# Values of one pair of heads after each round in the last five groups of attention

## What is computed

```python
def _L0_attn_ref(x, w_qkv, w_out, b_out):       # x: (8, 512, 256), H = 16
    qkv = x @ w_qkv
    q, k, v = jnp.split(qkv, 3, axis=-1)
    ...                                         # heads, rotation of q and k
    dots = jnp.einsum('bhid,bhjd->bhij', q, k) * scale
    attn = jax.nn.softmax(dots, axis=-1)
    out = jnp.einsum('bhij,bhjd->bhid', attn, v)
    ...
    return out @ w_out + b_out
x = x + _layernorm(_L0_attn_ref(_layernorm(x, axis=-1), ...), axis=-1)
x = x + _layernorm(_L0_ffn_ref(_layernorm(x, axis=-1), ...), axis=-1)
```

## Time and profile before

| | |
|---|---|
| time, median of 3 runs | 923.57 us (922.79 to 928.46) |
| the profiled execution | 924.53 us, span 921.5 us |
| mean granted TensorE clock | 0.945 |
| busy in the span | PE 777.2 us, DVE 654.4, ACT 519.5, POOL 377.2 |
| attends | 128, from 81.5 to 557.05 us |
| groups 27 to 31, from the last attend of group 26 | from 490.17 us |

### The profile page before, as it was taken

How to read it: one execution, slowest core, us unless ns; L and a number is a source line. 1 busy time by engine, 2 the same in 40 slices (tenths; PEclk the granted TensorE clock), 3 DMA queues, 4 the chain that set the end, 5 groups by cost and what they waited for, 6 DMA issues and landing times. The chain is left out here.

```text
span 921.5 us, 14947 instructions
## 1 busy us (share of the span) xinstructions
PE 777.2 (84%) x4690; PEld 482.1 (52%) x4690; DVE 654.4 (71%) x1252; ACT 519.5 (56%) x1050; POOL 377.2 (41%) x446
## 2 busy tenths in 40 slices
PE   4478899999999999999968877999999788888784
PEld 3344334344443344433422335787787688887673
DVE  4367778888888787987868844777875355554685
ACT  2214566767667676677747763434342376665363
POOL 4350071361632714418101010456566067666442
PEclk9657899999999999999979997999999899999998
DMA  8584925847739468286563401345447546556994
GB/s 154 115 223 96 221 48 128 192 112 146 161 101 196 93 145 191 95 173 116 130 170 59 185 1 49 98 144 161 150 156 220 144 136 183 170 171 204 283 174 91
DMA packets 112420, 133.27 MB, mean 145 GB/s; under 512 B 16724, under 2 KB 80726, under 8 KB 112344
## 3 DMA queue, kind: packets, MB, share of 16 engines
q1 hardware_dynamic: 99096, 109.18, 48.1%
q0 software_dynamic: 13248, 23.15, 9.7%
HBM read 68.18 MB, written 59.87 MB: 139 GB/s over the span
## 5 line engine op out<-in xcount | busy, mean ns | idle before, releaser
L460 DVE TENSOR_REDUCE negmax<-ring 128x2 f32<-128x1024 f32 x256 | 307.1, 1212 | 82.9 <-PE ring L615 81.5
L413 ACT ACTIVATE probs<-scores 128x512 f32<-128x512 f32 x498 | 272.3, 601 | 74.6 <-PE scores L631 73.5
L631 PE MATMUL scores<-q_st,k_st 64*128 64x512 f32 x498 | 208.2, 471 | 42.4 <-ACT probs L413 36.3
L615 PE MATMUL ring<-k_st,q_st 48*128 48x512 f32 x512 | 182.7, 469 | 9.2 <-DMA k_st<-rows_in 4.8
L631 PEld LDWEIGHTS scores<-q_st,k_st 64*128 64x128 f32 x498 | 83.0, 187 | 183.1 <-ACT probs L413 131.9
L643 PE MATMUL av<-probs,v_aug 128*32 128x512 f32 x1024 | 139.0, 615 | 6.3 <-ACT probs L413 6.3
L318 POOL CAST part_r<-negmax 128x16 fp32r<-128x16 f32 x32 | 8.4, 262 | 189.0 <-DVE negmax L460 189.0
L615 PEld LDWEIGHTS ring<-k_st,q_st 48*128 48x128 f32 x512 | 69.8, 193 | 16.8 <-DVE negmax L460 8.1
L1485 POOL DMA_INDIRECT rows_out<-m_y,projected x48 | 47.3, 985 | 45.7 <-ACT m_y L1550 35.1
L564 PE MATMUL misc<-projected,t_hi 128*128 128x512 f32 (+1 forms) x236 | 64.8, 365 | 0.0
L1636 DVE TENSOR_TENSOR m_h_lo<-scores,m_h_hi 128x512 fp32r<-128x512 f32 x40 | 27.7, 691 | 51.4 <-ACT m_h_hi L1536 51.3
(11 more groups left out here) (240 smaller groups left out, 1678.7 us busy)
## 6 DMA issues: line engine op xcount, KB each, us to landing
q_st<-rows_in SPq DMA_DIRECT2D x96, 128.0 KB, 4.4
k_st<-rows_in SPq DMA_DIRECT2D x96, 128.0 KB, 5.3
experts<-split SPq DMA_DIRECT2D x8, 1024.0 KB, 5.7
projected<-records SPq DMA_DIRECT2D x48, 129.0 KB, 2.4
split<-O SPq DMA_DIRECT2D x24, 256.0 KB, 6.0
experts<-rows_out SPq DMA_DIRECT2D x10, 512.0 KB, 6.5
m_rows<-records SPq DMA_DIRECT2D x32, 129.0 KB, 2.3
X<-in_x SPq DMA_DIRECT2D x8, 512.0 KB, 9.3
```

The lines of the kernel that those rows point to most:

```text
L413: nc.scalar.activation(probs[r // 2 % 2][r % 2][:, a, :], score_of(R)[:, a, :], ACT.Exp, scale=HD ** -0.5).then_inc(exp_done, 1)
L460: nc.vector.tensor_reduce(negmax[Gn % 2][:, t, 2 * p:2 * p + 2], ring[t % 2][:, :, :], AX.X, ALU.max, negate=True).then_inc(max_done, 1)
L615: last = nc.tensor.matmul(half[:, a, :], q[rows, t * P:(t + 1) * P], k[rows, :], start=True, stop=True)
L631: nc.tensor.matmul(score_of(R)[:, a, :], k[rows, kt * P:(kt + 1) * P], q[rows, :], start=True, stop=True).then_inc(sc_ps, 1)
```

## The change

`av_at` returns the pairs as well. Up to group 26 nothing differs: both pairs in every second round. In groups 27 to 31 the pair of each round is attended in the round behind it: pair 0 in odd rounds, pair 1 in even ones. `attend` waits for the exponentials of its last pair only, and signals `av_ps` once for each key block, behind pair 1, as before. The last call, behind all rounds, has pair 1 alone.

```diff
+    BY_PAIR = NGT - 5
+
     def av_at(G, r):
 
-        if r % 2:
+
+        before = G * 8 + r - 1
+        Ga, kt, p = before // 8, before % 8 // 2, before % 2
+        if not 0 <= Ga < NGT or Ga < BY_PAIR and p == 0:
             return None
-        Ga, kt = (G, r // 2 - 1) if r else (G - 1, QT - 1)
-        return (Ga, kt) if 0 <= Ga < NGT else None
+        return Ga, kt, (0, 1) if Ga < BY_PAIR else (p,)
...
-        def attend(G, kt):
+        def attend(G, kt, pairs):
             b, g = G // NG, G % NG
-            pe.wait_ge(exp_done, G * 16 + kt * 4 + 4)
-            if kt == 0:
+            pe.wait_ge(exp_done, G * 16 + kt * 4 + 2 * pairs[-1] + 2)
+            if kt == 0 and pairs[0] == 0:
...
-            for i in range(GH):
+            for i in [2 * p + a for p in pairs for a in range(2)]:
...
-            last.then_inc(av_ps, 1)
+            if pairs[-1] == 1:
+                last.then_inc(av_ps, 1)
...
-        attend(NGT - 1, QT - 1)
+        attend(NGT - 1, QT - 1, (1,))
```

## The result

The changed kernel takes 929.28 us, median of 20 runs (925.31 to 932.33), the kernel before 923.23 on the same chip; the ratio is 1.0061 with a 95% interval of 1.0042 to 1.0079, that is 5.6 us (3.9 to 7.3). The forecast was 929.4 in 922.5 to 934.5. A second series gave 926.82 against 924.88, ratio 1.0041 (1.0007 to 1.0074), 3.8 us (0.6 to 6.8). Ratios and their intervals leave out the executions that were over 1.5% slower than the fastest of their kernel, medians do not, so a ratio here need not be the quotient of the two medians. The profiled execution took 928.91 us, span 927.1 (before 924.53 and 921.5).

A forecast was written before the change was run, and what follows sets the result against it. A ring of PE and ACT was taken to bound the kernel before, PE the changed one. First 26 rounds +4.8, last 14 rounds +1.9, clock -0.9 sum to 5.8 us, forecast 929.4 us, range 922.5 to 934.5.

The forecast's parts named there:

- A pair costs what four heads cost: PE, attends of groups 27 to 31: two heads take 0.99 us to the next score matmul, as four heads do.
- PE becomes the bound, 1.66 and 1.42 a round: PE sets the pace: first 26 rounds 26 x 1.66 = 43.2 us, in the last 14 rounds 13 x 1.42 = 18.5.
- The wait for the bank `av`: A group's first pair waits until DVE has read the bank: 1.8 us in groups 27 to 30, 0.5 in 31.
- The small transposes: Transposes of the maxima, before in PE's pause, add 3 x 0.28 = 0.8 us in the first 26 rounds.
- ACT's casts: Casts on ACT delay the exponentials that PE needs: 0.5 us in group 29, 0.6 in group 31.
- First stretch and tail together: First 26 rounds +4.8 us (46.3 against 41.5), last 14 rounds +1.9 (25.4 against 23.5).
- The clock, -0.9: Last attend: with nearly no pause on PE the granted clock holds, where it had fallen before: -0.9 us.
- The total: Whole kernel: 4.8 + 1.9 - 0.9 = 5.8 us slower, 929.4 us.
- The range: Whole kernel: inner part 925.5 to 933 us, 0.07 a round to both sides and the clock; widened to 922.5 to 934.5.
- The half-price pair: Rival, chance 0.08: any four records run side by side, a pair takes 0.54 us; first stretch -3, tail -2.5, kernel 918.1.
- The pauses take it: Rival, chance 0.12: next score matmuls hide in a pair's second passes, rounds 1.52 to 1.6 us; +1 to +2, 925.
- DVE becomes the ring: Rival: natural matmuls wait for DVE's maxima, 0.7 us more in five groups, 933; chance 0.10, shared with larger layout costs.

The follow-up runs named there:

- first two experiments: Changed kernel with each pair's attend issuing four matmuls into four strips: one run 933.36 us; changed kernel with both heads of a pair in one strip: 956.47 us.
- second traces: Kernel before and changed kernel, both unaltered, traced again: from the last attend of group 26 to the last attend 64.94 and 70.01 us.
- the halves: Against the changed kernel, all four heads for half the queries each round in the last five groups: 919.63 us, kernel before 924.88, ratio 0.9930.
- the last two runs above: Kernel before with half-query attends from group 27, whole attends a round later in the tail: 958.71 us; half-query attends in all groups: 977.19; kernel before 963.62.

## Why the prediction was right, step by step

- **A pair costs what four heads cost.** Right: 0.98 to the next score matmul, forecast 0.99. The first two experiments show the reason that I had argued from the earlier trace rows: strips side by side, passes of one strip in a row. This was the term on which the sign hung.
- **PE becomes the bound, 1.66 and 1.42 a round.** Right: 1.65 and 1.41, read from before rows where nothing was waited for. 43.2 was forecast; 26 x 1.65 = 42.9, and the last of these rounds has no natural matmuls and takes 1.41 (533.85 to 535.26), which the sum overlooked: 42.7.
- **The wait for the bank `av`.** Right in place and releaser: 0.33 once and 0.44 three times, 1.65 in all, for 1.8; in the tail 0.56 for 0.5.
- **The small transposes.** 0.21 each, not 0.28: the scores behind one start before it has ended. 0.2 less.
- **ACT's casts.** In group 29 0.3 for 0.5 (528.13 to 530.09, 1.96 in place of 1.65). In group 31 nothing for 0.6: here the step failed. The cast falls into the round in which PE waits for the bank `av`. The next exponentials, due 0.59 behind the score matmuls of 551.11, would begin at 551.70; the cast had ended by 551.71. I had added two delays of the same round where only the longer one counts. That is most of why the tail cost +1.16 and not +1.9.
- **First stretch and tail together:** +5.06 for +6.7.
- **The clock, -0.9.** Wrong in place and size. I read one fall of the clock, 0.5 us ahead of the last attend, as what that tail brings. Three traces with this tail have it once ahead of the last attend and twice behind it. That a dense tail holds the clock was right: with pairs in the tail it fell 3.6 to 4.0 us behind the start of the last attend, in three traces of three. What the change gets from it in every trace is not the 0.9 in the last attend but 0.7 just behind the block, which I had not forecast; the 0.9 come on top only where the old tail loses its clock early, once in three traces.
- **The total.** 5.8 was forecast, 5.6 (3.9 to 7.3) measured; what the traces repeat is 5.06. Measured on to the L830 matmuls behind the block, with what the clock gives back, it is 4.3, or 3.4 where the old tail loses its clock early; both series' intervals hold 4.3. So the nearness of 5.8 to 5.6 is in part luck: the costs of the stretch were counted too high by 1.6, and the times scatter by more than that. In the first two profiled executions the difference of 5.6 in the spans is made up otherwise: -0.3 ahead of the stretch, +5.1 in it, -0.9 by the clock in the last attend, -0.7 by the clock behind the block, and +2.5 behind that, of which the second traces show nothing.
- **The range.** Its inner part, 925.5 to 933, is 929.4 with 2.8 to both sides and the clock; the clock had been taken off already, so the lower end should have been 926.6. Nothing hung on it.
- **Rivals.** The half-price pair is excluded by the first two experiments. "The pauses take it" is out: the round is 1.65, not under 1.6. "DVE becomes the ring" is out as well: no natural matmul waited for `negmax` on PE in these groups, DVE itself waits 0.4 for PE in nearly each round (503.78). The experiment with half the queries does bring DVE to the bound, at rounds of 1.24.

## What to carry to other kernels

Matmuls here whose outputs fill different strips cost together nearly what two of them cost (1.07 for four heads, 1.05 for two), so work on them is to be cut along the moving columns, never by strips: the same split in two cost 5.1 us here by heads and saved 4.5 by queries. Cutting a blocking piece pays a fixed part for each further piece (0.16 here), so count the engine's pauses first: in the first 26 rounds here PE stood idle 6.3 of 41.5 us and the halves saved 2.4, and with halves in all groups its last pauses were gone and the kernel came out slower. And ahead of an in-order engine's wait ask whether the waiting piece can stand behind work that needs the same signal: moving four heads one round later took 4.2 us off a tail of 23.5 with no work removed.

## What I had not expected of the hardware

- The granted clock of one and the same tail fell 0.5 us ahead of the last attend in one trace and 1.8 to 2.0 us behind its start in two others. A difference of 0.9 us between two single traces that hangs on such a fall is not evidence on a change. The time until the clock rises again, and with it 0.7 us of work behind the block, did go with the tail in all six traces.
- The start of the stretch differs between traces of one kernel by far more than its length: 490.17 and 496.32 us, lengths 64.95 and 64.94. This distance repeats to 0.01 us, where times need 20 runs for an interval of 0.2%; but not every distance does: from the first attend to the last it is 473.6 us in one trace of the kernel before and 480.2 in the other.
- The kernel before takes 923.23, 925.11 and 924.88 us in three series and 963.62 in a fourth, on another chip. In the two traces from that chip (the last two runs above) the last attend starts at 553.58 and 561.78, about where it does in the kernel before, and the part behind attention, which no run changes, takes 401.9 and 409.0 us where the other ten traces have 358 to 367; why is open.
